# The output projection's bias leaves TensorE and is added to x on VectorE; stores of the ranked list at other beats; the variance's constants as immediates

## What is computed

```python
def _L0_attn_ref(encodings, W_attn, b_attn, W_out, b_out):
    qkv = encodings @ W_attn + b_attn
    q, k, v = (to_heads(t) for t in jnp.split(qkv, 3, axis=-1))
    scores = jnp.einsum('bhki,bhqi->bhkq', k, q) / math.sqrt(HEAD)
    attn = softmax(where(mask, scores, -10000.0), axis=2)
    out = jnp.einsum('bhkq,bhkl->bhql', attn, v).transpose(0, 2, 1, 3).reshape(b, n, HIDDEN)
    return out @ W_out + b_out
x = _layernorm(x + _L0_attn_ref(x, ...))
x = _layernorm(x + _L0_ffn_ref(x, ...))     # top-k of x @ w_router, gelu MLP, scaled, scattered back
```

## Time and profile before

| | us |
|---|---|
| median of 3 runs | 2519.99 (2518.46 to 2521.81) |
| the profiled execution | 2524.1, its span 2522.4 |
| PE busy | 2459.1 (97%) |
| DVE busy | 1693.6 (67%) |
| ACT busy | 1218.1 (48%) |
| POOL busy | 1499.1 (59%) |

### The profile page before, as it was taken

The page is one execution under the profiler, slowest core; times in us unless marked ns, Lnnn a source line. Parts: engine busy times, 40 slices in busy tenths (PEclk is TensorE's granted clock), DMA queues, the critical chain, the costliest instruction groups (busy, mean ns, idle before and its releaser), DMA issues. The chain is left out here.

```text
span 2522.4 us, 40914 instructions
## 1 busy us (share of the span) xinstructions
PE 2459.1 (97%) x14168; PEld 1815.3 (72%) x14168; DVE 1693.6 (67%) x4334; ACT 1218.1 (48%) x2191; POOL 1499.1 (59%) x1438
## 2 busy tenths in 40 slices
PE   8999999999999999999999999998999999999997
PEld 6656677777677777677667667764788888888886
DVE  7767778778777777777888787775655544553533
ACT  3655566666566666666666566666421111111110
POOL 2877778777877787777778777775233122221311
PEclk9999999999999999999999999998999999999999
DMA  4233435335344443444434344443421001010000
GB/s 176 90 127 119 148 140 199 123 127 184 135 149 156 144 148 136 173 141 155 160 132 149 126 160 144 144 152 97 167 76 43 17 26 43 26 34 26 28 24 17
DMA packets 167502, 287.45 MB, mean 114 GB/s; under 512 B 23241, under 2 KB 58121, under 8 KB 166026
## 3 DMA queue, kind: packets, MB, share of 16 engines
q1 hardware_dynamic: 160130, 267.99, 30.4%
q0 software_dynamic: 7168, 16.85, 2.1%
HBM read 116.97 MB, written 65.11 MB: 72 GB/s over the span
## 5 line engine op out<-in xcount | busy, mean ns | idle before, releaser
L869 POOL TENSOR_TENSOR Pa<-Pa,Pm 128x512 f32<-128x512 f32 (+1 forms) x602 | 747.5, 1267 | 110.7 <-ACT Pm L981 97.2
L1478 PE MATMUL PS<-Kp,Qp 128*128 128x512 f32 (+3 forms) x1536 | 487.4, 352 | 12.7 <-DVE nm L1093 10.0
L1512 PE MATMUL PS<-Qp,Kp 128*128 128x512 f32 (+3 forms) x1536 | 492.1, 356 | 7.7 <-ACT Pm L981 3.3
L981 ACT ACTIVATE Pm<-PS 128x512 f32<-128x512 f32 (+1 forms) x643 | 358.1, 568 | 257.3 <-PE PS L1512 207.6
L1093 DVE TENSOR_REDUCE nm<-PS 128x1 f32<-128x512 f32 x512 | 344.2, 686 | 151.3 <-PE PS L1478 151.0
L869 POOL TENSOR_TENSOR Pa<-Pa,P 128x512 f32<-128x512 f32 (+1 forms) x297 | 370.0, 1271 | 53.3 <-ACT P L981 46.6
L1478 PEld LDWEIGHTS PS<-Kp,Qp 128*128 128x128 f32 x1536 | 277.9, 190 | 113.5 <-issue 37.3
L943 ACT ACTIVATE G<-PS,b1c 128x512 f32<-128x512 f32 x128 | 88.2, 689 | 539.7 <-PE PS L1565 539.6
L1101 DVE CUSTOM_DVE_ANT_0 PS<-PS,maskA 128x384 f32<-128x384 f32 (+3 forms) x512 | 246.2, 508 | 147.8 <-PE PS L1478 146.7
L1512 PEld LDWEIGHTS PS<-Qp,Kp 128*128 128x128 f32 x1536 | 276.3, 190 | 92.5 <-ACT Pa L981 28.9
L1101 DVE CUSTOM_DVE_ANT_0 PS<-PS,maskA,nm 128x384 f32<-128x384 f32 (+3 forms) x512 | 264.4, 553 | 80.9 <-PE PS L1478 76.9
(11 more groups left out here) (159 smaller groups left out, 4229.1 us busy)
## 6 DMA issues: line engine op xcount, KB each, us to landing
Qp<-nat SPq DMA_DIRECT2D x192, 256.0 KB, 2.5
Kp<-nat SPq DMA_DIRECT2D x192, 256.0 KB, 3.2
o_s<-Of SPq DMA_DIRECT2D x64, 256.0 KB, 2.2
Ot<-o_s SPq DMA_DIRECT2D x64, 256.0 KB, 3.1
xb<-in_x SPq DMA_DIRECT2D x64, 256.0 KB, 3.1
h_s<-hs SPq DMA_DIRECT2D x64, 256.0 KB, 2.3
out<-xb SPq DMA_DIRECT2D x64, 256.0 KB, 2.3
x_raw<-in_xt SPq DMA_DIRECT2D x15, 1024.0 KB, 6.4
```

Source lines behind the costliest of these rows:

```text
L869: e.tensor_tensor(to, to, probs(u, k)[:, h0:h0 + many, 0:w], ALU.add).then_inc(s["padd"], many)
L981: e.activation(probs(u, k)[:, hh[0]:hh[-1] + 1, 0:w], tile_bank(j)[:, 0:len(hh) * w].rearrange("p (h n) -> p h n", n=w), ACT.Exp).then_inc ...
L1478: ins = e.matmul(to, Qp[:, u % 4, h_, qt * P:qt * P + P], Kp[:, (2 * i + k0 // 512) % 4, h_, 0:w], start=True, stop=True)
L1512: ins = e.matmul(tile_bank(j)[:, x_ * w:x_ * w + w], Kp[:, (2 * i + k // 4) % 4, h_, k % 4 * P:k % 4 * P + P], Qp[:, u % 4, h_, 512 - w:51 ...
```

## The change

The thirteenth matmul is gone; an O job now has twelve, and the last is given two ticks, so that the job still fills thirteen ticks. The last matmul is the one at what was tick 12 of the job, so `T.beat` of the first 53 O jobs is one beat smaller (phase 13 and 29 in place of 14 and 30), and with it everything keyed on it; for the last 11 it is unchanged. CB becomes a plain tile with the bias row spread over all 128 partitions: SP writes `crow` to memory and reads it back broadcast, once, at the start. DVE adds CB to each loaded tile of x, one TENSOR_TENSOR of two SBUF tiles of 128x512 per O job, four beats after SP's load of it (phases 5 and 21) or one beat before the job's last. The evacuation waits for that add (`x_bias`) in place of the load. The variance becomes two TENSOR_SCALARs with immediates, the `lnc` tiles go. The list is stored at phases 0 and 13 of four pairs (beats 832, 845, 864, 877, 896, 909, 928, 941). SP waits for the last add before it loads b2B, which lies over CB.

```diff
-PIECES = {"K": [1] * 12, "Q": [1] * 12, "V": [1] * 12, "O": [1] * 13, "T": [2], ...}
+PIECES = {"K": [1] * 12, "Q": [1] * 12, "V": [1] * 12, "O": [1] * 11 + [2], "T": [2], ...}
...
+        o_add = {}
+        for load in o_load:
+            for j in o_load[load]:
+                o_add.setdefault(min(load + 4, T.beat[j] - 1), []).append(j)
...
-        list_beat = {max(rank_beat) + 5 + 12 * t: t for t in range(TT)}
+        LIST_AT = (0, 13)
+        first_pair = -(-(max(rank_beat) + 5) // (2 * BEATS))
+        list_beat = {2 * BEATS * (first_pair + t // 2) + LIST_AT[t % 2]: t for t in range(TT)}
...
+                if n == T.beat["C",] + 2:
+                    e.wait_ge(*freed(("C",)))
+                    e.dma_start(cD[:, :], crow).then_inc(s["cb_st"], 16)
+                if n == T.beat["C",] + 5:
+                    e.wait_ge(s["cb_st"], 16)
+                    e.dma_start(CB[:, :], cD[0].rearrange("(a n) -> a n", a=1).broadcast_to([P, D])).then_inc(s["cb_in"], 16)
...
                     ff_load(7)
+                    e.wait_ge(s["x_bias"], len(T.o_jobs))
                     e.dma_start(b2B[:], b2.rearrange("(a n) -> a n", a=1).broadcast_to([P, D])).then_inc(s["fc"], 16)
...
-                    link(e.tensor_tensor(crow, src[0:1, :], crow, ALU.add))
-                    linked()
-                    link(e.tensor_copy(CB[0:1, :], crow))
-                    linked()
-                    e.tensor_tensor(CB[96:97, :], crow, CB[0:1, :].bitcast(F32), ALU.subtract).then_inc(s["ev_v"], 1)
+                    e.tensor_tensor(crow, src[0:1, :], crow, ALU.add).then_inc(s["ev_v"], 1)
                 else:
                     o = o_number(job)
                     y = xb[:, o % 2, :]
                     e.wait_ge(*done(job))
-                    e.wait_ge(s["xb", o % 2], 16 * (o // 2 + 1))
+                    e.wait_ge(s["x_bias"], o + 1)
                     e.tensor_tensor(y, src, y, ALU.add).then_inc(s["ev_v"], 1)
...
-                        e.scalar_tensor_tensor(out=lvar[:, k, :], in0=lnc[:, 0, :], scalar=lmv[:, k, 1:2],
-                                               in1=lnc[:, 1, :], op0=ALU.mult, op1=ALU.add)
+                        e.tensor_scalar(lvar[:, k, 0:1], lmv[:, k, 1:2], EPS, 1.0, ALU.add, ALU.mult)
+                        e.tensor_scalar(lvar[:, k, 1:2], lmv[:, k, 1:2], 1.0 + EPS / 4, EPS * EPS / 4, ALU.mult,
+                                        ALU.add)
...
+                for j in o_add.get(n, ()):
+                    o = o_number(j)
+                    if o == 0:
+                        e.wait_ge(s["cb_in"], 16)
+                    e.wait_ge(s["xb", o % 2], 16 * (o // 2 + 1))
+                    e.tensor_tensor(xb[:, o % 2, :], xb[:, o % 2, :], CB[:, :], ALU.add).then_inc(s["x_bias"], 1)
...
-                    if k < 12:
-                        term, kt = divmod(k, KT)
-                        oh, wh = ((0, 0), (1, 0), (0, 1))[term]
-                        ins = e.matmul(to, Os[:, oh, kt, :], Wo[wh][:, kt, :], start=k == 0, stop=False)
-                    else:
-                        ins = e.matmul(to, ones[0:97, :], CB[0:97, :], start=False, stop=True)
+                    term, kt = divmod(k, KT)
+                    oh, wh = ((0, 0), (1, 0), (0, 1))[term]
+                    ins = e.matmul(to, Os[:, oh, kt, :], Wo[wh][:, kt, :], start=k == 0, stop=k == 11)
```

More of the change, by code:

```diff
@@ L157, in dense_jobs @@
     return jobs
-PIECES = {"K": [1] * 12, "Q": [1] * 12, "V": [1] * 12, "O": [1] * 13, "T": [2], "S": [1], "N": [4], "C": [4] * 4}
+PIECES = {"K": [1] * 12, "Q": [1] * 12, "V": [1] * 12, "O": [1] * 11 + [2], "T": [2], "S": [1], "N": [4], "C": [4] * 4}
 TICKS = 54
@@ L433, in layer @@
         xT = (sb("xTh", [P, KT, N], F32R), xTl)
-        CB = sb("CB", [P, D], F32R)
+        CB = sb("CB", [P, D], F32)
         Qp = sb("Qp", [P, 4, 4, 512], F32R)
@@ L456, in layer @@
             "lnnb", [P, 2, 2], F32)
-        lvar, lmean, lnc = sb("lnvar", [P, 2, 2], F32), sb("lnmean", [P, 2, 1], F32), cs["lnc"]
+        lvar, lmean = sb("lnvar", [P, 2, 2], F32), sb("lnmean", [P, 2, 1], F32)
         li = sb("li", [P, 2, 4, 2], U32)
@@ L473, in layer @@
         bA, sc, sg = cs["battn"], cs["sc"], cs["sg"]
-        hD, scD, wD, oD = dr["h"], dr["sc"], dr["wqkv"], dr["o"]
+        hD, scD, wD, oD, cD = dr["h"], dr["sc"], dr["wqkv"], dr["o"], dr["cb"]
         xr = x.rearrange("b (t p) d -> b t p d", p=P)
@@ L784, in gpsimd @@
             e.memset(cs["minus"][:], -1.0).then_inc(s["c0"], 1)
[L785 to L789, removed]
+            e.wait_ge(s["c0"], 5)
             e.affine_select(out=cs["identf"][:], in_=cs["identf"][:], compare_op=ALU.not_equal, fill=1.0, base=0,
@@ L797, in gpsimd @@
             e.iota(cs["tok"][:], pattern=[[P, TT]], base=0, channel_multiplier=1).then_inc(s["c0"], 1)
-            e.memset(CB[:, :].bitcast(F32), 0.0).then_inc(s["ones"], 1)
             e.memset(ones[:, :].bitcast(F32), 1.0).then_inc(s["ones"], 1)
@@ L1277, in vector @@
                 if n == 0:
-                    e.wait_ge(s["c0"], 13)
-                    e.wait_ge(s["ones"], 2)
+                    e.wait_ge(s["c0"], 9)
+                    e.wait_ge(s["ones"], 1)
                     e.wait_ge(s["rk0"], 1)
@@ L1390, in wait_ready @@
                         e.wait_ge(s["wo_lo"], 2)
-                        e.wait_ge(*freed(("C",)))
                 if d >= 2:
@@ L1641 @@
 SEMAPHORES = ("c0", "bias", "b_scaled", "wq_in", "w1_in", "x0_hi", "rk0", "w_in", "w_hi", "w_split", "w_st", "v_in", "v_hi", "v_split", "v_st", "wo_in",
-              "wo_hi", "wo_lo", "x_hi", "x_lo", "ones", "rows", "d_mm", "ev_v", "ev_a", "kq_hi", "a_mm", "a_max",
+              "wo_hi", "wo_lo", "cb_st", "cb_in", "x_bias", "x_hi", "x_lo", "ones", "rows", "d_mm", "ev_v", "ev_a", "kq_hi", "a_mm", "a_max",
               "shift", "b_mm", "b_exp", "keep", "padd", "pv", "o_cp", "nln", "rinv", "ot", "os_hi", "os",
@@ L1655, in program @@
         "sc": nc.dram_tensor("sc_s", [B, N], F32).ap(),
+        "cb": nc.dram_tensor("cb_s", [1, D], F32).ap(),
         "o": nc.dram_tensor("o_s", [B, P, KT, N], F32).ap(),
@@ L1670, in program @@
             "half": sb("half", [P, 2], F32), "minus": sb("minus", [P, TT], F32),
-            "lnc": sb("lnc", [P, 2, 2], F32),
             "sc": sb("sc", [P, B, TT], F32), "sg": sb("sg", [P, B, TT], F32),
```

## The result

The median of after is 2550.49 us (2548.05 to 2552.3), of before 2520.30 (2518.46 to 2521.81) on the same chip: ratio 1.0117, interval 1.0104 to 1.0129. After is slower by 30.2 us; I had said 19. In the profiled executions the spans are 2550.6 and 2522.4, 28.2 apart; all that follows is made against these.

The account below looks back on a forecast made before the run. PE, busy 97%, was taken as the bound; 15.3 + 3.3 - 2.1 + 3.5 - 0.8 = +19.2 us on the median 2519.99 gave 2539 us, slower by 0.8%, range 2526 to 2555 to hold 8 in 10.

Parts of the forecast that it names:

- Part 1, the matmul: Removed bias matmul on PE: gain 0 in odd slots, where PE waits for ACT, at most 0.1 us in even.
- Part 2, normal pairs: Evacuation one beat earlier, ahead of A 14.18 on DVE: F 0.73 us later per even slot, 21 pairs, +15.3 us.
- Part 2, x pairs: F 1.25 us later, up to 1.0 back from POOL's mask wait, add +0.4: 0.65 each, five pairs, +3.3 us.
- Part 3, the adds: 64 DVE adds, 0.7 us at phase 5, 1.2 at 21, hidden in DVE's waits: 0, at worst +0.5 a slot.
- Part 3, rank pairs: DVE's rank counting one beat earlier, at phase 24 ahead of a piece with less slack: +0.7 each, five pairs, +3.5 us.
- Part 4: Variance and list: stall after the stretched L1308 goes, -0.8 us; x split caught again behind beat 877's store, 0.
- The tail: Last 11 O jobs keep their beat; nine stand between matmuls that wait for nothing, 0.23 us each: -2.1 us.
- (a): Rival at F: A 14.18 is reduced before PE gets there, so the evacuation's shift is hidden; 2514 to 2518, chance 0.12.
- (b): Rival: (a) with the stall at beat 877 gone as well, 4.3 us faster; 2510 to 2513, chance 0.05.
- (c): Rival: POOL becomes the bound at phase 28, held back 0.7 us by each add; 14 on top, 2553, chance 0.1.
- (d): Rival: adds cost less, F more given back in x pairs, rank pairs 0; 2525 to 2533, within the forecast's 0.73.

Follow-up runs that it names:

- evac_later: After with DVE's evacuation of the first 53 O jobs put back one beat, behind A 14.18, the matmuls left as in after; 2537.43 us in one execution.
- keep_beat: After with the two ticks given to the eleventh matmul of an O job, so the last matmul is back in before's beat; 2519.01 us, ratio to before 0.9987.
- no_add: After without the 64 DVE adds, the output projection's bias left out of the result; 2544.93 us in one execution.
- rank_back: After with DVE's rank counting and ranking one beat later, at phases 25 and 9 as in before; 2550.15 us in one execution.
- var_list: Before with only the variance by constants and the list stores at after's beats, the bias matmul kept; 2520.48 us against 2521.74.
- moved_both: keep_beat with the adds of the first 53 jobs at phases 7 and 29 and the list stores at phases 31 and 0; 2505.08 us, ratio to before 0.9935.
- no_matmul: Before without the thirteenth matmul, the twelfth on the last tick so all beats stay, bias left out; 2509.09 us, ratio 0.9946.

## Why the prediction came out as it did

Sign and range were right; the middle was 11 us too low, 9 by the traces. By its steps:

- **Part 1, the matmul.** Odd slots 0, measured 0.00 (the 0.65 us from ACT to the B tile unchanged). Even slots at most 0.1, measured 0.01 in evac_later. Right, but only for after's hole; I had not asked what another place of it would give (0.46 a pair, keep_beat).
- **Part 2, normal pairs.** F was late by 0.71, predicted 0.73, for the reason given. Two things beside it were not in the sum. ACT normalises the tile one beat sooner: +0.11 by phase 9, and waits of together 0.22 us at phase 18 go (below). In the pairs 9, 13, 17 the transpose of scores (S, L1498) waits for DVE, +0.4. Over the eleven pairs 6 to 20 that are no x pairs they cancel: 8.0 measured, 8.0 predicted. The two short waits, in before, PE, its weight loads, and then ACT:

```profile
300.58 0.39 PE L1478 MATMUL PS<-Kp,Qp 128*128 128x512 f32 x1
300.93 0.50 PE L1512 MATMUL PS<-Qp,Kp 128*128 128x512 f32 x1
301.26 0.86 PE L1424 MATMUL PS<-xTh,Wkh 128*128 128x512 f32 x3
```

```profile
300.93 0.19 PEld L1512 LDWEIGHTS PS<-Qp,Kp 128*128 128x128 f32 x1 [0.38 <-ACT Pm L981]
```

```profile
299.59 0.80 ACT L1044 ACTIVATE xb<-xb,lnnb,lnrs 128x512 f32<-128x512 f32 x1
300.30 1.06 ACT L981 ACTIVATE Pm<-PS 128x512 f32<-128x512 f32 x2
```

The steps between PE's starts are 0.35 and 0.33 us. In after they are 0.22 and 0.23, and ACT has finished the tile long before:

```profile
298.83 0.39 PE L1485 MATMUL PS<-Kp,Qp 128*128 128x512 f32 x1
299.05 0.39 PE L1519 MATMUL PS<-Qp,Kp 128*128 128x512 f32 x1
299.28 0.84 PE L1434 MATMUL PS<-xTh,Wkh 128*128 128x512 f32 x3
```

- **Part 2, x pairs.** 1.63 each, predicted 0.65, bound 1.7. F was right (1.22 against 1.25), the add was right (0.4). The step that was wrong is the wait of PE for POOL that was to be given back ("POOL's chain doesn't hang on F there, so up to that much comes back"): no_add shows F late by its full amount and POOL's wait still 0.98. Missing: 1.0 a pair, 4 us in pairs 7 to 19.
- **Part 3, the adds.** 0 in normal pairs, measured 0.04, though each takes up to 1.1 us longer than its 0.69. Their sum is 72.8, outside the 50 to 65 I gave, and the lengths are the wrong way round: 1.75 at phase 5 and 0.68 at phase 21. I had looked at how busy POOL is at phase 21, and not at where in one of its sums the add would begin.
- **Part 3, rank pairs.** The term that was mis-sized most: these five pairs grew by 13.2 where my terms for them give 7.1 (3.5 for ranks). The adds make 6.1 of it, a term that stood at 0 there, and the list's chain in pair 25 is most of the rest. The reason I gave, counting at a beat of less slack, with +0.7 a pair, fails in four of the five pairs (rank_back: 0.15 to 0.3 in three, 1.7 the other way in the fourth). That the counting's 3.5 us is near the 3.0 that rank_back gives back in sum is luck: 4.0 of it is the list's chain in pair 25.
- **Part 4.** "Variance -0.8": the stall in pair 26 went, -0.96 in var_list and about -1.1 in after (-0.45 where a normal pair has +0.61). The size was right; that the variance's form did it, and not the store's new beat, isn't shown. The store at beat 877 "should be caught again": it was, 5.53 us. Shown with its price by moved_both: 3.6 us in pair 27, inside the bound of 4.3.
- **The tail.** -1.2 against -2.1; the runs put it anywhere from -1.2 to -3.7, so this isn't a difference that they tell.
- **The rivals.** (a) and (b) fall: F waits 28 times. (c) falls. Its premise was right in part: POOL was held back, by some 0.4 us an add (it is busy 21.0 us more than in before, and in pair 6 the mask operation behind the add of phase 21 takes 1.09 us where before's takes 0.69). But PE's wait for POOL's mask (L1537) dropped from 11.5 to 8.7 us. (d) had x pairs and rank pairs at nothing, and these two came out high.

Two small slips in the working change nothing: 400.44 - 399.17 is 1.27 and not 1.25, and the terms at their low ends add up to some 2525 us and not 2527.

Sum of the misses against 19.2: x pairs +3.9, rank pairs +6.1, pairs 26 to 31 +0.6, tail +0.9, start -2.5: +9.0, which makes the 28.2.

**The rule on SBUF.** An add that begins 0.07 us behind a POOL sum takes 1.75 us in place of 0.69. The Trainium skill, "SBUF — State Buffer", section "SBUF: two separate sides", says that a DVE operation with two SBUF inputs and a GpSimd operation that reads SBUF exclude each other for a whole instruction. By that rule the extra is at most the rest of one sum; the rest is 1.21 us here, and 1.06 agrees. The 5.53 us above don't: they span four sums, so there DVE waited through several instructions. In moved_both no split is that long, the store being elsewhere; why DVE waits so long behind a store was not settled.

Open: why pair 23 gains 2.9 us from the adds' absence and loses 1.7 in rank_back. It is the one pair that is both x and rank pair, and no run takes the two apart. Open too are pair 27's -2.3 in no_matmul against -0.9 in keep_beat, and its -1.02 in var_list, where the split was caught just as long. Not told apart are the adds' length and their place in DVE's order, and the variance's form and the store's beat.

## To carry to other kernels

When work is taken out of an order written by hand, ask where the hole lies. At the end of a job in front of a wait it gained nothing here, and it let the job's end fall one beat earlier, so that two steps of DVE went ahead of a reduction that PE was about to need (0.7 us in each normal pair, 1.2 in an x pair); one beat before, the same hole gained 0.23 us in each slot. An operation that two engines' use of SBUF can stretch is placed by the other engine's timeline: in keep_beat's order the same adds cost 9 to 10 us more at phases 5 and 21 than at phases 7 and 29, where in pairs 6 to 25 they cost nothing that the traces show.

## What was not expected of the hardware

- A vector add of 128x512 with both inputs in SBUF took 0.66 to 1.78 us. It depended on where in a POOL sum it began: 0.07 us behind its start it took 1.06 us longer, 0.12 us ahead of its end nothing; in between, the rest of the sum less about 0.14 us.
- The tiny steps of the list are stretched as well: L336 (128x8) took 0.98 us in after where its shortest is 0.16, while POOL finished its fourth sum in a row.
- After one DMA issue of POOL (L352), at beat 877 or 878, a split of x took 5.51 to 6.18 us in each of the nine kernels with a store there, for 0.68 of work; without the store there 1.81 at most.
- The two scalar steps that replace the one with two SBUF inputs take 0.15 us each and were never stretched (142 to 146 ns for the second), though POOL was as busy beside them: in var_list most of them begin 0.67 to 0.77 us before the end of a POOL sum and take 0.14 to 0.16, where L1308 of before, begun 0.75 to 0.77 before the end of the same sum, took 0.76 to 0.78 in place of its 0.22. No run has them right behind a store.
